# A batch group's last attention head: row maxima alone in the first pass, row sums from a column of ones, and its blocks interleaved with the next group's first head

## The reference

```
for i in range(H):
    att = jnp.einsum('btd,bsd->bts', q_rot, k_rot) * scale
    if cascade_bias is not None:
        att = att + cascade_w[i - 1] * cascade_bias
    att = softmax(where(causal, -inf, att))
    head_outputs.append(jnp.einsum('bts,bsd->btd', att, v[:, i]))
    cascade_bias = jnp.mean(att, axis=1, keepdims=True)     # mean over the queries: one number a key
```

## Time and profile before

| | us |
|---|---|
| median of three runs | 3336.99 (3334.38 to 3339.17) |
| span of the profiled execution, all that the profile shows of it | 3451.7 |
| the first to the last exponential of the attention | 47 to 3236 |
| behind it: last group's finishing, routing, experts | 216 |
| busy in the span: PE / ACT / DVE / POOL | 3126 / 3085 / 2614 / 2148 |

### The profile page before, as it was taken

One profiled execution on the slowest core, in us unless ns is written; L12 is line 12 of the kernel. 1 busy time (PEld: TensorE's weight loads), 2 busy tenths in 40 slices (PEclk: granted clock), 3 DMA queues, 4 the chain that ended last, 5 costly groups with the idle time before them and its releaser, 6 DMA issues. The chain is left out here.

```text
span 3451.7 us, 93100 instructions
## 1 busy us (share of the span) xinstructions
PE 3126.0 (91%) x29688; PEld 1529.3 (44%) x29688; DVE 2614.4 (76%) x7854; ACT 3085.3 (89%) x8904; POOL 2147.9 (62%) x6194
## 2 busy tenths in 40 slices
PE   6899999989999989998999999998999998898955
PEld 3333333333444434454445444444444543444644
DVE  7666666666877787887888887787888877777754
ACT  4999999999999999998999999998999999888724
POOL 5666666665666367776666677775667655565345
PEclk9999999999999999999999999999999999999986
DMA  5322322232333324343444423344434333344353
GB/s 162 97 86 72 88 71 71 74 88 79 90 101 107 103 78 127 117 122 109 131 115 124 120 84 94 114 116 131 117 93 123 113 101 84 105 121 145 110 187 125
DMA packets 270525, 370.74 MB, mean 107 GB/s; under 512 B 61654, under 2 KB 177118, under 8 KB 270033
## 3 DMA queue, kind: packets, MB, share of 16 engines
q1 hardware_dynamic: 254784, 326.39, 32.4%
q0 software_dynamic: 14976, 37.34, 3.7%
q10 hardware_dynamic: 272, 1.05, 0.1%
HBM read 259.76 MB, written 104.40 MB: 106 GB/s over the span
## 5 line engine op out<-in xcount | busy, mean ns | idle before, releaser
L1490 DVE CUSTOM_DVE_ANT_0 att_a<-scores,window 128x128 f32<-128x128 f32 (+7 forms) x2048 | 1489.6, 754 | 464.9 <-PE scores L1182 307.7
L1356 ACT ACTIVATE att_a<-att_a,neg_max 128x128 f32<-128x128 f32 (+7 forms) x2048 | 1593.0, 778 | 73.3 <-DVE neg_max L1490 69.5
L1366 ACT ACTIVATE att_t<-scores 128x1024 f32<-128x1024 f32 (+7 forms) x2048 | 1329.5, 649 | 88.6 <-PE scores L1200 61.1
L1198 PE MATMUL scores<-q_stack,k_stack 104*128 104x512 bf16 (+3 forms) x3072 | 822.5, 333 | 130.1 <-DVE neg_max L1490 74.7
L1216 PE MATMUL pv<-att_t,v_sb 128*32 128x256 f32 (+7 forms) x16384 | 917.9, 300 | 5.7 <-ACT att_t L1366 3.3
L1182 PE MATMUL scores<-k_stack,q_stack 99*128 99x512 bf16 (+3 forms) x3072 | 687.7, 331 | 67.1 <-ACT att_t L1366 39.1
L1216 PEld LDWEIGHTS pv<-att_t,v_sb 128*32 128x32 f32 x16384 | 328.9, 108 | 592.9 <-issue 549.0
L1198 PEld LDWEIGHTS scores<-q_stack,k_stack 104*128 104x128 bf16 x3072 | 258.4, 98 | 531.2 <-DVE neg_max L1490 233.9
L1200 PE MATMUL scores<-identb,mask 128*128 128x128 bf16 x2048 | 454.7, 222 | 0.0
L1816 POOL TENSOR_SCALAR biasv<-col_sum,w_cas 128x8 f32<-128x8 f32 x240 | 88.8, 370 | 552.9 <-ACT att_t L1366 540.2
L1366 ACT ACTIVATION_READ_ACCUMULATOR att_t<-scores 128x1 f32 x2048 | 424.0, 207 | 0.0
(11 more groups left out here) (345 smaller groups left out, 4342.8 us busy)
## 6 DMA issues: line engine op xcount, KB each, us to landing
runner_r<-in_experts SPq DMA_DIRECT2D x137, 384.0 KB
qk_parts<-of_proj SPq DMA_DIRECT2D x128, 384.0 KB
of_proj<-in_xt SPq DMA_DIRECT2D x29, 1024.0 KB
q_stack<-qk_parts SPq DMA_DIRECT2D x256, 96.0 KB
k_stack<-qk_parts SPq DMA_DIRECT2D x256, 96.0 KB
q_stack<-qk_parts SPq DMA_DIRECT2D x256, 64.0 KB
k_stack<-qk_parts SPq DMA_DIRECT2D x256, 64.0 KB
head_out<-o_sb SPq DMA_DIRECT2D x252, 64.0 KB
```

What stands on the lines that cost most here:

```text
L1198: engine.matmul(scores[:, c0:c1], ks[0:ROWS_B, j * P:(j + 1) * P], qs[0:ROWS_B, j * P + c0 - base:j * P + c1 - base], start=True, stop=True)
L1356: engine.activation(taken, taken, EXP, scale=-1.0, bias=neg_max[:, n, i:i + 1], accum_out=row_sum[:, n, i:i + 1]).then_inc(s_exp_a, 1)
L1366: engine.activation(att_t[:, ring:ring + end - base], scores[:, base:end], EXP, accum_out=col_sum[:, n, j:j + 1]).then_inc(s_exp_b, 1)
L1490: engine.tensor_tensor_reduce(out=att_a[:, ring:ring + end - base], in0=scores[:, base:end], in1=window[:, T - (end - base):T], op0=ALU.ad ...
```

## The change

The 16 units of the last heads are `bare`. Nobody needs their column sums, and their row sums are taken another way:
- Pass A of a bare unit is `fill_a` and `take` alone: no `exp_a`, `guess`, `egl`, `parts`, `lack`. DVE writes the block back to `scores`. POOL splits the maxima into three bf16 parts (`plain`, six small instructions).
- Pass B of a bare unit takes exp of scores minus maximum, without an accumulator. The value columns beside the last head hold ones (`v_ones` on POOL, or the 1.0 behind the last block), so `pv`, which always multiplied 32 columns, gives the row sums on partitions 16 to 31 of each strip. `o_move` becomes three instructions of DVE: shuffle the sums over, reciprocal, multiply.
- The steps are laid out by `lay_steps`. Around each of three group borders nine steps become five: with U the next group's first unit they do `A(U) A(U-4) B(U-6)`, `A(U+1) A(U-3) B(U-5) B(U-4)`, `A(U+2) A(U-2) B(U) B(U-3)`, `A(U+3) A(U-1) B(U+1) B(U-2)`, `A(U+4) B(U+2) B(U-1)`. At the end of the last group they are `A(251) A(252) B(249)`, `A(253) B(250)`, `A(254) B(251)`, `A(255) B(252)`, `B(253)`, `B(254)`, `B(255)`.
- Counters of semaphores are by the new sequences. The planner's other rules are those of before.

```diff
+    def bare(u):
+        return coords(u)[1] == NH - 1
+    def lay_steps():
+        steps = []
+        for u in range(UNITS):
+            g, n = divmod(u, PER_GROUP)
+            if bare(u):
+                continue
+            if g and n < SLOTS:
+                takes = [u, u - SLOTS]
+                b = [[u - 6], [u - 6, u - 5], [u - 2, u - 5], [u - 2, u - 5]][n]
+            elif g and n == SLOTS:
+                takes, b = [u], [u - 2, u - 5]
+            else:
+                takes, b = [u], [u - 2] if u >= 2 else []
+            steps.append(Step(takes, u, b))
+        end = UNITS - SLOTS
+        steps[-1].takes.append(end)
+        steps += [Step([end + 1], None, [end - 2]), Step([end + 2], None, [end - 1]), Step([end + 3], None, [end])]
+        steps += [Step([], None, [end + k]) for k in range(1, SLOTS)]
+        return steps
...
+    def lay_rows():
+        jobs = []
+        for step in STEPS:
+            on = [u for u in step.b if not bare(u)]
+            if step.a is None:
+                jobs += [(None, w) for w in on] + [(u, None) for u in step.takes]
+                continue
+            jobs += [(u, None) for u in step.takes if bare(u)]
+            jobs.append((step.a, on[0] if on else None))
+        return jobs
...
+                if bare(u):
+                    engine.activation(att_t[:, ring:ring + end - base], scores[:, base:end], EXP).then_inc(s_exp_b, 1)
+                    return
...
+                if bare(u):
+                    dve.wait_ge(s_dve, chained(engine.stream_shuffle(moved, pv[:, 0:2 * P], SUMS)))
+                    dve.wait_ge(s_dve, chained(engine.reciprocal(moved, moved)))
+                    engine.tensor_tensor(moved, pv[:, 0:2 * P], moved, ALU.mult).then_inc(s_oev, 1)
+                else:
+                    engine.tensor_copy(moved, pv[:, 0:2 * P]).then_inc(s_oev, 1)
...
+            def plain_of(u):
+                low, left = neg_max[:, 2, :], rest[:, 0, :]
+                pool.wait_ge(s_max, a_done(u, TB - 1))
+                small(engine.memset(bits[:, shift_at + NPART * TB:TURNED], 0.0))
+                ev = small(engine.tensor_copy(part(shift_at, 0), low))
+                pool.wait_ge(s_small, ev)
...
+                engine.tensor_tensor(part(shift_at, 2), left, part(shift_at, 1), ALU.subtract).then_inc(s_shifted, 1)
```

542 lines of the change are left out of this document (335 added, 207 removed).

## The result

The changed kernel takes 3392.19 us (median, 3383.57 to 3399.65) where the kernel before takes 3338.08 (3334.38 to 3339.99) beside it on the same chip: ratio 1.0161, 95% interval 1.0142 to 1.0181. Forecast were 3300 us and a range of 3262 to 3338.

What follows compares the result with a forecast made beforehand. ACT was taken as the first bound, with PE and DVE close behind. 346.7 - 283.5 - 11 - 8.5 - 6 = 38 us of the trace, times 0.967, is 37 of the median 3337: 3300 us, range 3262 to 3338.

Steps and rivals of the forecast that it cites:

- What bounds the kernel now: Attention steps: ACT is the first bound, busy 11.10 of 11.10 us without side work; PE and DVE stand close behind.
- A bare unit saves 6.9 us of ACT, 16 of them 110: Bare units: dropped exponentials and cheaper accumulator-free ones save 6.9 us of ACT each, 110 us for 16.
- What DVE gets: Bare unit's move on DVE: 3.0 us against 0.42, bounds 1.4 to 3.4, with the reciprocal taken as 2.0.
- The three borders: Group borders: nine steps become five, full steps 19.5 us; together 283.5 us for 346.7, a gain of 63.
- Rival 3: Borders: the shared bank's hand-over replaces ACT as bound, full steps take 24 us, total about 3338; chance 0.17.
- Side work moved elsewhere, 11 and 8.5 us: Outside the borders: 33 displaced PE stages cost 11 us, and stalls falling anywhere in a new order 8.5.
- The end: Last group from unit 252's first exponential: 66 us against 65.7, saved exponentials spent on waiting, so nothing is won.
- Rival 4: End: three waits idle PE and its clock falls, up to 46 us more, then 3345 us; chance 0.10.
- the sign written down, waits over 10 us each: Last group's end: the prediction called itself wrong if the waits there exceed 10 us each.
- The tail, +6 us: Behind the last `pv`: 210 PE stages against 192, 18 x 0.9 x 0.36 = 6 us more.
- The factor 0.967: Final sum: 38 us of the 3451.7 us trace, times 0.967, become 37 us of the 3337 us median.

Runs made afterwards that it cites:

- e15: Kernel before's finished orders with the bare units' mathematics, two buffers of maxima, and the move as a single copy (last head not divided): ratio 0.9971 to the kernel before.
- e13: Kernel before's finished orders with the bare units' mathematics, the long three-instruction move and two buffers of maxima: ratio 1.0099 to the kernel before.
- e6_after_again: The changed kernel run again, nothing altered, beside the kernel before on one chip: ratio 1.0164.
- e10: Kernel before with one planner cost nudged (guess 0.30 us instead of 0.28), no instruction added or taken: ratio 1.0114 to the kernel before.
- e11: Changed kernel with one planner cost nudged (DMA landing 1.65 us instead of 1.6), no instruction added or taken: ratio 1.0085 to the kernel before.
- e1_base: The kernel before, unchanged, traced on the slower kind of chip: 3447 us.
- e2: Changed kernel with only the end put back to its old steps, woven borders kept, planned anew: ratio 1.0129 to the kernel before.
- e4: Changed kernel's mathematics with the old step order everywhere, side work laid anew by the planner: ratio 1.0083 to the kernel before.
- e7: Changed kernel's mathematics in the old step order, planner told a bare unit still takes its first exponentials' time: ratio 1.0132 to the kernel before.
- e8: Kernel before with the last three tiles of each of group 2's four runners held until the last exponential: ratio 1.0058 to the kernel before.
- e5_base_again: The kernel before, unchanged, traced on the faster kind of chip, the same kind as the changed kernel's trace: 3341 us.

## Why the prediction was wrong, step by step

- **What bounds the kernel now.** Right as far as it goes: a step without side work is ACT's, 11.2 us. The prediction says that the other two "stand close behind it". How close is what the runs add: `e15` shows where a step stops when ACT is taken away: at 9.9, PE's 8.7 and its waits.
- **A bare unit saves 6.9 us of ACT, 16 of them 110.** Right for ACT (93 us less busy), wrong as time by a factor of ten: on the unchanged order, with the most favourable move, all sixteen are worth 9 us (`e15`).
- **What DVE gets.** The size was right: reciprocal 1.75 us (2.0 taken, 1.4 to 3.4 for the whole move, measured 2.7 from 805.0 to 807.7). The Trainium skill's page "VectorE: DVE Perf Modes", section "First, the fixed hardware budget", states a repeat count of 8, from which 2.1 us was estimated; the trace shows 1.75, fixed part included, so the measurement decides. Takes written back to PSUM took 772 ns instead of 753, 2.4 us in all, and not 60 ns more. What failed is its weight: priced as one of several sums in a step, it cost 1.28% of the whole kernel on the order of before (`e13` less `e15`, 42 us for 16 moves, 2.6 us each for 2.3 of DVE's time), by way of PE's gaps and its clock.
- **The three borders, "I take 19.5 for a full step, 1.5 over DVE's sum".** This is the step that failed, twice. The steps took 19.0, 21.0, 21.3, 21.2 and 18.8 for 14.5, 19.5 three times and 17.5: 10.8 us at the first border, 34.7 over the three (318.2 for 283.5). Of the 10.8 us 4.5 are in the first step, 5.0 in the three full ones. The full step was summed on the wrong engine: DVE's 18.0 and 1.5 for queues. DVE was busy 17.3, not over 90% of the step. The step was PE's 18.8, which the prediction had as 18.9, and 2.3 of PE's waits, for the move (1.2) and for exponentials (1.1); 19.5 leaves 0.6 for them. In the first step PE was busy 14.8 of 19.0 us and waited 2.7 for takes and 1.6 for exponentials, where 14.5 left nothing for waits. At the other borders the full steps took 20.8 to 23.7. And what they replaced was read on the slower kind of chip: 346.7 us there, 324.5 on the kind that the forecast is for, 22.2 less to win. Of the gain of 63 there was 6.3 left. Rival 3, the shared bank's hand-over in ACT's place, had the outcome of the borders nearly right (full steps at 24, hardly any gain), but not the mechanism: in a full step PE waits for the exponentials of pass B only 1.1 us, and the rest of the step is PE's work and the move.
- **Side work moved elsewhere, 11 and 8.5 us.** Measured 28 in the stretches between, and 22 in the second run of the changed kernel (`e6_after_again`, unit 251's first exponential 15.7 us later than before). The size is near the forecast's 19.5, but that side work is the cause is not shown. `e10`'s nudge moved unit 251's start by 4.9 us only, so the order's luck as `e10` shows it is too small for this; the changed kernel's own nudge leaves it (`e11` starts unit 251 20.3 us later than `e1_base`). The pair `e2` and `e4` puts 18 us on the woven borders, while `e7`, with the old borders and another cost for a bare unit, is 32.7 late at the same place. This part of the loss stays open.
- **The end, "nothing is won".** Its place and mechanism were right, its size wrong: 94.2 us where before took 74.2. The full step with two passes A before the waits (18.6 us for 11.7) was costed nowhere. The first wait was 13 us and not 9.2 less 1: POOL does the split of unit 252, its work for 251 and the bias for one row job (from 3114.6 to 3120.9), and behind the landing the fill stands on PE behind tile work at the lower clock. Rival 4 described this and was given 0.10. It asked for 13 us at each of three waits; there was one of 13.2, and two of 6.6 and 6.0, so the sign written down, waits over 10 us each, came for the first alone.
- **The tail, +6 us.** Measured 16.5, for six more tiles. The 0.36 us per us of PE was taken from the attention, where tiles lie under ACT; `e8` gives 2.4 us a tile behind it and 0.45 under it.
- **The factor 0.967.** I took it for a profile that runs slower than a plain execution. It is another chip: spans are within 6 us of the medians wherever both are of one chip.
- **The rivals.** That the time lies above 3344 was given 0.11, and the only rival that reached so far was rival 4, the end, with 3345. None had all three losses at once: borders that win nothing, an end 20 us longer and a tail 16 us longer. Two small slips in the sums move nothing: 11.6 us over four jobs are 2.9 each and not 2.7, and rival 3 has half of its chance below 3330 in one place and a third in the other.

## What to carry to other kernels

- An engine that is 100% busy in a step is its bound only down to the next one, and the next one's pace is its work plus its own waits: here 9.9 us against 11.2, so of 6 us taken from ACT 1.3 were won. Before work is taken off it, run the step without that work (and without what replaces it): here this one run (`e15`) would have said 0.3% at best before anything else was written.
- What replaces the work must be asked where it stands in an in-order queue. 2.7 us in front of the takes and of PE's next product cost more than their length where PE ran dry and its clock read 0.50; 1.4 us at the same place, with PE released after 0.45 of them, cost next to nothing in these steps.
- If a planner lays out the whole program, compare an edit on the finished order of before first, and run the kernel once with a planner cost moved by a hair: that difference (here 1.1% slower for one kernel, 0.8% faster for the other) is the noise of every comparison between two plans. And look where it lies: in `e10` it was in the end and the tail.

## What the runs showed of the hardware

- Two kinds of chips, 3.2% apart on the unchanged kernel (3447 us in `e1_base`, 3341 in `e5_base_again`), equal in quiet stretches (first border 104.7 and 104.6 us) and apart where side work and DMA are dense (third border 117.3 and 107.7, tail 215.0 and 189.3). With it the granted clock at that border is 0.96 on the slower and 1.00 on the faster kind. Each chip was used in one set of runs only, so that it is the chip, and not something that held for the length of a set, is not shown.
- A reciprocal of 128x256 on DVE takes 1.753 us, one of 128x8 0.203; a transpose of 128x256 in 32x32 squares takes 0.445 us, from PSUM as well as in place in SBUF, hardly more than the copy's 0.42.
